# A four-layer graph network on one core: VectorE's chains dealt out between its one-hot tiles in the typed gather stage

## The reference

```python
h = softplus(softplus([x[r], edge_attr] @ W1 + b1) @ W2 + b2) @ W3 + b3   # layer 0, then segment_sum
msg = Ht[edge_type, edge_src]; m_agg = segment_sum(msg, edge_dst)         # layer 1, typed messages
gi = m_agg @ w_ih.T + b_ih; gh = h @ w_hh.T + b_hh                        # then a GRU per node
r = sigmoid(i_r + h_r); z = sigmoid(i_z + h_z); n = tanh(i_n + r * h_n)
new = (1.0 - z) * n + z * h
i1 = einsum('ecb,eb->ec', inter, basis); tanh(i1 @ ii_W1 + ii_b1)         # layer 2, then segment_sum
mean = segment_sum(x[src], dst) / clip(cnt, 1); mean @ W_l + b + x @ W_r  # layer 3, two convolutions
```

## Time and profile before

| what | value |
|---|---|
| time, median of 3 runs | 8726.32 us (8710.41 to 8737.31) |
| profiled execution, its own time | 8717.75 us |
| its span in the profile | 8716.2 us |
| TensorE, VectorE, ScalarE, GpSimd busy over the span | 84%, 62%, 42%, 46% |
| mean granted TensorE clock | 0.874 |

### The profile page before, as it was taken

One profiled execution on the slowest core, in us unless ns is written; L12 is line 12 of the kernel. 1 busy time (PEld: TensorE's weight loads), 2 busy tenths in 40 slices (PEclk: granted clock), 3 DMA queues, 4 the chain that ended last, 5 costly groups with the idle time before them and its releaser, 6 DMA issues.

```text
span 8716.2 us, 178254 instructions
## 1 busy us (share of the span) xinstructions
PE 7332.7 (84%) x38529; PEld 3642.1 (42%) x38529; DVE 5424.6 (62%) x17512; ACT 3644.4 (42%) x6136; POOL 4014.8 (46%) x4668
## 2 busy tenths in 40 slices
PE   6999999766666666666667999999999899999999
PEld 5777777422222222222223444444444444444443
DVE  7888888677777777777765777777777312121111
ACT  6999999554444444444442333333333000000000
POOL 4333333376566566656656777777776000000000
PEclk9999999866666666666668999999999999999999
DMA  4333333422222222222222222222222555556665
GB/s 123 96 97 97 96 97 96 149 89 78 78 76 79 79 82 78 79 74 81 77 77 54 61 61 61 61 62 61 60 60 54 153 166 170 166 152 203 192 192 174
DMA packets 873624, 880.18 MB, mean 101 GB/s; under 512 B 219482, under 2 KB 694599, under 8 KB 873255
## 3 DMA queue, kind: packets, MB, share of 16 engines
q1 hardware_dynamic: 720119, 732.67, 26.8%
q0 software_dynamic: 115440, 129.86, 7.6%
q10 hardware_dynamic: 37760, 14.89, 0.7%
HBM read 650.07 MB, written 227.66 MB: 101 GB/s over the span
## 4 chain that ended last, share of the span: by engine, by line
PE 66%; DVE 15%; issue 10%; POOL 3%; ACT 3%; DVEq 2%; DMA 1%; ACTq 0%; SPq 0%; POOLq 0%
PE ps L2306 12%; PE ps L2183 7%; PE ps L2311 6%; PE ps L1982 6%; PE ps L2147 6%; PE ps L2000 5%; PE ps L2007 4%; PE ps L2175 4%; POOL zone L950 3%; DVE zone L1534 3%; DVE zone L1533 2%; ACT zone L1849 2%; PE ps L2202 2%; DVE zone L1280 2%; PE ps L1998 1%
## 5 line engine op out<-in xcount | busy, mean ns | idle before, releaser
L950 POOL DMA_INDIRECT zone<-tab_msg,idx x1664 | 1788.9, 1075 | 1091.2 <-DVE idx L1211 656.7
L2147 PE MATMUL ps<-zone 128*128 128x396 bf16 x3200 | 1135.3, 463 | 896.0 <-DVE zone L1534 724.8
L950 POOL DMA_INDIRECT zone<-tab_u,idx x1664 | 1586.4, 953 | 587.2 <-issue 477.8
L1849 ACT ACTIVATE zone<-ps 128x792 fp8e4<-128x792 f32 x1600 | 1250.0, 828 | 1289.8 <-PE ps L2147 1287.3
L1280 DVE TENSOR_TENSOR zone<-ps,zone 128x512 f32<-128x512 f32 x1664 | 1064.3, 686 | 362.9 <-PE ps L2175 335.5
L2306 PE MATMUL ps<-zone 128*128 128x512 fp8e4 x4900 | 1154.9, 381 | 22.8 <-DMA zone<-adj 13.9
L1534 DVE TENSOR_SCALAR zone<-tT,zone 128x392 bf16<-128x392 f16 x3200 | 1014.1, 317 | 0.0
L2147 PEld LDWEIGHTS ps<-zone 128*128 128x128 bf16 x3200 | 307.7, 105 | 1570.0 <-issue 839.9
L1533 DVE TENSOR_SCALAR zone<-tT,zone 128x128 bf16<-128x128 f16 x3200 | 804.1, 251 | 224.0 <-PE ps L2147 220.1
L1982 PE MATMUL ps<-zone 128*128 128x64 f32 (+1 forms) x6656 | 833.5, 280 | 113.3 <-DMA zone<-tab_msg,idx 94.0
L2183 PE MATMUL ps<-zone,w_bas 128*64 128x512 f32 x3328 | 899.3, 619 | 0.0
(11 more groups left out here) (306 smaller groups left out, 9731.6 us busy)
## 6 DMA issues: line engine op xcount, KB each, us to landing
zone<-adj SPq DMA_DIRECT2D x350, 768.0 KB, 4.6
adj<-zone SPq DMA_DIRECT2D x200, 784.0 KB
zone<-in_dst_row SPq DMA_DIRECT2D x832, 128.0 KB, 2.6
zone<-in_ea_T SPq DMA_DIRECT2D x416, 128.0 KB, 2.5
zone<-src_lin SPq DMA_DIRECT2D x3264, 0.5 KB
zone<-adj SPq DMA_DIRECT2D x50, 896.0 KB, 4.8
tab_msg<-zone SPq DMA_DIRECT2D x104, 256.0 KB, 2.1
zone<-tab_msg,idx POOLq DMA_INDIRECT x1664
```

The source lines that it names most:

```text
L950: nc.gpsimd.indirect_dma_start(out=gat(e, u)[:, k, :], out_offset=None, in_=table, in_offset=bass.IndirectOffsetOnAxis(ap=idx[:, u, k:k + ...
L1849: nc.scalar.activation(staging[m % 2][:, :, at_ * 2 * WN:(at_ + 1) * 2 * WN].rearrange("p b (w d) -> p w b d", w=2), pair_[:, :, 0:CX].rea ...
L2147: mm(bank(4 + w % 4)[:, 0:CX], hot_lo[w % HOTS], hot_hi[w % HOTS], start=True, stop=True) \
```

## The change

Six edits, all but one in the typed stage:

- The chains of VectorE (`decode`, `update` with `norm_group`) become generators. `begin` issues the first operation; `advance`, called after each of the two one-hot builds of a window, issues the next one. What is left is issued at the next `begin`, before the codes are copied and at the turn's end. In groups with a constant number (after the loop) they run as before.
- The pieces come one step later: candidate at step 3, update at 4, TensorE's turn at 6, its multiplication at 7, u and v at the end of the turn. Decode comes one step earlier (3), and the turn of the codes too (5).
- ScalarE copies the u and v rows instead of VectorE, at the end of its turn, and has one more move of windows between sigmoid and tanh; SyncE stores these rows after all 8 parts of slots instead of after five.
- The loops of `chunk_loop`, on every engine that uses it and in the three stages, are built with `hint_back_edge=True`, which tells the engine ahead of time where its loop branch goes.
- The ring of one-hot tiles has 16 pairs instead of 4.

```diff
-HOTS = 4
+HOTS = 16
+        def announced(eng, first, end):
+            return nc.Fori(first, end, engines=bass.OrderedEngineSet([eng.engine]), hint_back_edge=True)
@@ chunk_loop
-            with eng.Fori(peel, from_turn) as it:
+            with announced(eng, peel, from_turn) as it:
                 turn(it, False)
             if from_turn < ITERS:
-                with eng.Fori(from_turn, ITERS) as it:
+                with announced(eng, from_turn, ITERS) as it:
                     turn(it, True)
@@ SyncE, turn()
-                        if uv and part == 5:
-                            store_rows(gru_of, it - behind, turn0, [tab_u, tab_v], lambda g: rows_out)
+                    if uv:
+                        store_rows(gru_of, it - behind, turn0, [tab_u, tab_v], lambda g: rows_out)
@@ VectorE
+            running = []
+            def advance():
+                if running and next(running[0], "over") == "over":
+                    running.pop()
+            def finish_running():
+                while running:
+                    advance()
+            def begin(chain, alone):
+                finish_running()
+                running.append(chain)
+                advance()
+                if alone:
+                    finish_running()
@@ norm_group (each call of it: yield from after(...))
                 def after(ins):
                     ins.then_inc(ordered, 1)
+                    yield
                     dve.wait_ge(ordered, flow_value(flow, "ordered", turn0, g, n[0]))
...
                 def update(g):
                     wait_flow(dve, f, "shaped", t0_, g, 1)
+                    begin(updating(g), isinstance(g, int))
...
-                def rows_uv(g):
-                    wait_flow(dve, f, "formed", t0_, g, 2)
-                    wait_free(dve, f, t0_, g)
-                    nc.vector.tensor_copy(rows_out, by_block(bank(0)[:, 0:SB * H])).then_inc(f.sems["settled"], 1)
-                return [(2, candidate), (3, update), (7, rows_uv)]
+                return [(3, candidate), (4, update), (RING, lambda g: finish_running())]
...
                 def decode(it):
...
+                    begin(decoding_of(it), isinstance(it, int) and it < 2)
...
                 def take_codes(it):
+                    finish_running()
                     dve.wait_ge(codes_turned, groups0 + it)
...
                             nc.vector.tensor_scalar(hot_lo[w % HOTS], iota_h[:, 0:P128], codes[:, w:w + 1], None, ALU.is_equal)
+                            advance()
                             nc.vector.tensor_scalar(hot_hi[w % HOTS][:, 0:CW], iota_h[:, 0:CW], ...) \
                                 .then_inc(hot_built, 1)
+                            advance()
...
-                return ([(1, 4, False, decode), ...
+                return ([(1, 3, False, decode), ...
@@ ScalarE, gru_chain (typed stage)
                 nc.scalar.activation(gates, ..., ACT.Sigmoid)
+                move(2)
                 wait_flow(act, f, "mixed", turn0, g, 1)
                 nc.scalar.activation(cand, cand, ACT.Tanh)
-                move(2)
                 move(3)
                 move(4)
+                move(5)
                 (wait "turned" 1; lift of the new rows)
-                move(5)
+                move(6)
                 (wait "formed" 1; Tanh into tT)
-                move(6)
                 move(7)
+                wait_flow(act, f, "formed", turn0, g, 2)
+                wait_free(act, f, turn0, g)
+                act.sem_inc(act_turn, 1)
+                nc.scalar.activation(rows_out, by_block(bank(0)[:, 0:SB * H]), ACT.Copy).then_inc(f.sems["settled"], 1)
@@ TensorE
-                return [(1, turn_own), (2, gru), (5, turn_next), (6, pp1), (7, rows_uv)]
+                return [(1, turn_own), (2, gru), (6, turn_next), (7, pp1), (RING, rows_uv)]
-                           side=[(1, 6, False, turn_codes), ...
+                           side=[(1, 5, False, turn_codes), ...
```

More of the change, by code:

```diff
@@ L1383, in turn_base, with norm_group @@
                 return dve.snap(p * SG)
-            def norm_group(flow, turn0, g, first, to, squares):
+            running = []
[11 more added lines that the diff above has]
+                    finish_running()
+            def norm_group(flow, turn0, g, first, to, squares, done_as):
                 ordered = flow.sems["ordered"]
@@ L1398, in norm_group @@
                 dve.sem_inc(dve_turn, 1)
[L1399 to L1403, removed]
@@ L1404, in norm_group @@
-                after(nc.vector.tensor_scalar(stat[:, 1, :], stat[:, 1, :], 1.0 / D, EPS, ALU.mult, ALU.add))
+                yield from after(nc.vector.tensor_reduce(out=stat[:, 0, :], in_=rows, axis=AX.X, op=ALU.add))
+                yield from after(nc.vector.scalar_tensor_tensor(out=to, in0=stat[:, 0, :].unsqueeze(2).to_broadcast(small),
+                                                                scalar=-1.0 / D, in1=rows, op0=ALU.mult, op1=ALU.add))
+                yield from after(nc.vector.tensor_tensor(squares, to, to, ALU.mult))
@@ L1405, in norm_group @@
+                yield from after(nc.vector.tensor_reduce(out=stat[:, 1, :], in_=squares, axis=AX.X, op=ALU.add))
+                yield from after(nc.vector.tensor_scalar(stat[:, 1, :], stat[:, 1, :], 1.0 / D, EPS, ALU.mult, ALU.add))
                 var, root, step_ = (stat[:, n_, :] for n_ in (1, 2, 3))
-                after(nc.vector.tensor_scalar(root.bitcast(I32), var.bitcast(I32), 1, None, ALU.logical_shift_right))
-                after(nc.vector.tensor_scalar(root.bitcast(I32), root.bitcast(I32), -1.0, float(0x5F3759DF),
-                                              ALU.mult, ALU.add))
+                yield from after(nc.vector.tensor_scalar(root.bitcast(I32), var.bitcast(I32), 1, None, ALU.logical_shift_right))
@@ L1409, in norm_group @@
+                yield from after(nc.vector.tensor_scalar(root.bitcast(I32), root.bitcast(I32), -1.0, float(0x5F3759DF),
+                                                         ALU.mult, ALU.add))
                 for _ in range(3):
-                    after(nc.vector.tensor_tensor(step_, var, root, ALU.mult))
-                    after(nc.vector.scalar_tensor_tensor(out=step_, in0=step_, scalar=-0.5, in1=root,
-                                                         op0=ALU.mult, op1=ALU.mult))
@@ L1413, in norm_group @@
[L1413 to L1417, removed]
+                    yield from after(nc.vector.tensor_tensor(step_, var, root, ALU.mult))
@@ new lines, in norm_group @@
+                    yield from after(nc.vector.scalar_tensor_tensor(out=step_, in0=step_, scalar=-0.5, in1=root,
+                                                                    op0=ALU.mult, op1=ALU.mult))
+                    yield from after(nc.vector.scalar_tensor_tensor(out=root, in0=step_, scalar=1.5, in1=root,
+                                                                    op0=ALU.add, op1=ALU.mult))
+                nc.vector.scalar_tensor_tensor(out=to, in0=to, scalar=0.0, in1=root.unsqueeze(2).to_broadcast(small),
+                                               op0=ALU.max, op1=ALU.mult).then_inc(flow.sems[done_as], 1)
@@ L1443, in update @@
                                                    op0=ALU.mult, op1=ALU.add).then_inc(f.sems["ordered"], 1)
+                    yield
                     wait_flow(dve, f, "ordered", t0_, g, 3)
[L1445 to L1452 removed]
+                    yield from norm_group(f, t0_, g, 4, next_h, square, "normed")
+                return [(3, candidate), (4, update), (RING, lambda g: finish_running())]
             def sum_pieces(p):
@@ L1467, in norm3 @@
                 def norm3(g):
-                    norm_group(f, t0_, g, 1, h[:, bass.ds(g * SB, SB), :], square2).then_inc(f.sems["settled"], 1)
+                    begin(norm_group(f, t0_, g, 1, h[:, bass.ds(g * SB, SB), :], square2, "settled"), True)
                 return [(2, result), (3, norm3)]
@@ L1491, in decode, with decoding_of, after @@
                             nc.vector.memset(hot_hi[n][:, CW:CX], 1.0)
+                    begin(decoding_of(it), isinstance(it, int) and it < 2)
+                def decoding_of(it):
+                    def after(n):
+                        yield
+                        dve.wait_ge(decoding, (groups0 + it) * 6 + (n - 5))
                     nc.vector.tensor_copy(at_f.bitcast(I32), wsrc)
                     nc.vector.tensor_copy(st_f, st_i).then_inc(slots_taken, 1)
+                    yield
                     dve.wait_ge(slots_taken, (groups0 + it) + 1)
@@ L1497, in decode @@
                                             ALU.logical_shift_left).then_inc(decoding, 1)
-                    after(0)
+                    yield from after(0)
                     nc.vector.tensor_copy(lo_f, lo_f.bitcast(I32))
@@ L1501, in decode @@
                     nc.vector.tensor_scalar(ends, st_f[:, 1:WN + 1], st_f[:, 0:1], None, ALU.subtract).then_inc(decoding, 1)
```

(6 more changed lines are left out.)

12 lines of the change are left out of this document (7 added, 5 removed).

## The result

The changed kernel takes **8281.15 us** (median of 4 runs, 8277.53 to 8285.01) against 8725.73 us before (4 runs beside it); ratio 0.9493, 95% interval 0.9481 to 0.9504. Forecast was 8244, in a range of 8125 to 8430. The profiled execution took 8281.46 us. The forecast turn was 46.5 us, and it came out at 47.0. But what fills the turn is not what the prediction had filled it with.

What follows compares the result with a forecast made beforehand. The typed stage was taken as bound by VectorE's serial stretches; afterwards GpSimd's 44.2 us plus 2.3 for hand-overs give 46.5 us a turn against 56.8. Over 46 turns that gains 474 us: 8717.75 - 474 = 8244 us, range 8125 to 8430.

Steps and rivals of the forecast that it cites:

- the likeliest case: Typed stage: 45.3 to 48.5 us a turn with node work, 8190 to 8336 us, likeliest 8244; chance 0.42.
- hand-overs: Typed stage: 2.3 us a turn for hand-overs between four nearly equal engine chains, added to GpSimd's 44.2.
- Denser VectorE work might make it dearer: GpSimd's gathers in the typed stage: denser VectorE work might lengthen them, 1 us a turn either way.
- The gather is a wall: Rival: GpSimd's gathers set the typed stage's turn, everything else fits beneath; 44.2 us a turn, 8138 us; chance 0.22.
- VectorE, 40 us: VectorE's need per typed-stage turn after the change: 38.4 to 44.8 us, taken as 40.
- What the ring of 16 buys: One-hot tiles: VectorE up to 12 windows further ahead, 4.7 us, covering its branch and half of a chain.
- The announcement brings nothing: Rival: VectorE's loop branch keeps its 2.9 us; nothing if covered, exposed 133 us, 8377 us; chance 0.12.
- Coupling stays: Rival: VectorE stands for the sigmoid, chains stretch windows, TensorE waits again; 50.5 us a turn, 8428 us; chance 0.16.
- The slower rival: Loop branches of all three stages: announced targets are fetched each turn, 153 turns pay 595 us; 8839 us; chance 0.04.
- SyncE, 43 to 44: SyncE's need per typed-stage turn: loads and stores 40.8 us, with last slots' landing and branch 43 to 44.
- TensorE with ScalarE at 40: TensorE with ScalarE per typed-stage turn: 44 us at half clock or 34 at full, taken as 40.
- The clock: Clock granted to TensorE in the typed stage: to rise from 0.64 to 0.75 or more.

Runs made afterwards that it cites:

- Experiments 6: The changed kernel with three gathers per chunk in the typed stage in place of four, leaving out a quarter of the messages: 8123.20 us.
- 11: The changed kernel with a small VectorE instruction added between the two builds of each window in a turn's last two steps: 8230.23 us.
- 12: The changed kernel with a small VectorE instruction between the two builds of every window in which no chain runs: 8201.24 us.
- Experiments 2: The changed kernel with 4 one-hot tiles in place of 16: 8283.58 us.
- 9: The kernel before with 16 one-hot tiles and nothing else: 8742.12 us.
- experiments 4: The changed kernel with plain loops in place of the announced ones in all three stages: 8272.18 us.
- 10: The changed kernel with 4 one-hot tiles and plain loops: 8374.38 us.
- experiment 5: The changed kernel with 4 one-hot tiles, plain loops and every VectorE chain in one piece: 8477.87 us.
- 3: The changed kernel with every VectorE chain run to its end in one piece where it is begun: 8371.90 us.
- experiment 7: The changed kernel with both one-hot tiles built only 16 columns wide, leaving out most of the count matrix: 8049.79 us.

## Why the prediction was right or wrong

**The time and the turn** were right: 8281 for 8244, 47.0 us for 46.5, in the likeliest case's own range. That they came so close was luck.

**The sum behind it was right only by two errors that cancel.** It read 44.2 for GpSimd and 2.3 for hand-overs. Measured are 46.9 and 0.1. The mis-sized term is the gather: "Denser VectorE work might make it dearer", priced at 1 us a turn either way from the two means 1.049 and 1.080, was 2.6 us. It was also the sign I had named for being wrong ("if gathers lengthen beyond 1.15 us"). The trace of before showed it already in nine single gathers of 3.4 to 3.7 us, which a mean hides:

```profile
2388.56 3.37 POOL L950 DMA_INDIRECT zone<-tab_msg,idx  x1 [0.31 <-DVE idx L1211]
2446.68 3.74 POOL L950 DMA_INDIRECT zone<-tab_msg,idx  x1 [0.30 <-issue]
```

And the 2.3 us for hand-overs had no row behind them: the prediction's own case without node work showed 0.4, and the changed kernel 0.1.

**"The gather is a wall"** (0.22) was the right mechanism at the wrong price. GpSimd has no idle time but its issue gap. Experiments 6, 11 and 12 show that it sets the turn: fewer gathers, or shorter ones, shorten it, though only by some 3 us before VectorE and the ring set it.

**VectorE, 40 us** (38.4 to 44.8), was right: it waits for ScalarE and TensorE 183.1 + 137.9 us in 45 turns, so with its branch, as the prediction counts, it needs 47.0 - 7.1 = 39.9. The hidden chains are in it. The update runs from 2952.73 to 2960.92, 8.2 us with the builds going on beneath it, where it took 5.7 alone.

**"What the ring of 16 buys"** failed. It was to cover 4.7 us. Experiments 2 and 9 give nothing with it alone, either way round: in both pairs the gathers are longer with 16 tiles (1.080 to 1.162 us, 1.083 to 1.247), and with 4 tiles in the changed kernel VectorE waits for TensorE ahead of 126 builds (311 us between 1950 and 4050 us), which breaks its rows, with 16 hardly ever (3 us). Only with plain loops does it show (experiments 4 and 10: 102 us).

**"The announcement brings nothing"** (0.12) was wrong in its mechanism: the idle time went from 3.9 to 1.1 us. The rule of the Trainium skill that I had weighed there (Runtime: NRT & Kernel Launch, Instruction fetch mechanics) does not describe an announced back edge; the trace disagrees with it. On the time that rival was right in this kernel, and wrong in the kernel before (94 us).

**"Coupling stays"** is what experiment 5 shows at 51.3 us a turn: the later pieces alone. It goes away with the chains between the builds and one of the other two parts (experiments 2 and 4); with the chains' part or with the other two alone some 90 us are missing (10 and 3). The slower rival, a fetch at every loop, did not occur: 51 instruction packets in the whole kernel for 273.

**SyncE, 43 to 44**, was too high: with the same loads, stores and matmuls the turn was 42.0 us in experiment 7. TensorE with ScalarE at 40 isn't refuted by that; no run parts it from the rest. SyncE's wait for the decode, 676 us over the stage before, is 74, with 161 at the stores.

**The clock** was to rise to 0.75 and stood at 0.68, from 0.64: TensorE still has idle stretches of 3 to 5 us, now for gathered rows. It read 0.75 with three gathers and 0.79 with short builds.

**The small things**: the five chances of "faster by more" add up to 0.94, not 0.93. At nothing stood the three groups after the loop, where nine of the 12 us lie that the span lost against the turns.

## What to carry to other kernels

When every engine is nearly full, an edit is worth what the fullest engine gains from it: the announcement brought 94 us alone and nothing once GpSimd was saturated. Before pricing denser work on one engine, look at the longest instructions of the others, not at their mean. A few of three times the usual length, which all start beneath a row of one kind of instruction of another engine, point to one engine holding up the other; an edit that only changes that row, as in experiments 7 and 11, can show it. And an extra small instruction can pay, where it breaks up such a row.

## What the runs showed of the hardware

- GpSimd's gather of 128 rows takes 0.95 us, but some take 2.2 to 5.9 when VectorE's fp16-to-bf16 builds of 128 and 392 columns run back to back beneath them; with builds of 16 columns none of 763 took over 1.4. A 128x1 f32 operation in each window (0.065 us) left 4 of 716 over 1.9. One selection or sum every two windows did not do that.
- Being caught hangs on the moment too. In the changed kernel the caught gathers of a turn's last two steps all start 0.10 to 0.14 us behind the start of a 128-column build, while others at that offset are not caught (0.11 us into a row, for most of them, where the caught ones are 0.53 or 1.29 us into it). What exactly lets a caught gather go, I have not settled.
- An announced loop branch costs VectorE 1.1 us a turn where a plain one costs 3.9, and 4.5 once at the loop's entry.
